# A fused audio tower: the tokenizer's end in another order, its last stores waited for later, and 127 unread TensorE turns

## The reference

```python
def reference(x, ...):
    h = _L0_tok_ref(x, W, b, gamma, beta)            # 16x16 patches @ W + b, then layernorm
    h = h + _L0_attn_ref(_layernorm(h), Wq, Wk, Wv, Wo, bo)   # 16 heads of 64, rope, causal
    h = h + _L0_ffn_ref(_layernorm(h), router_w, router_b, w1, w3, w2)   # 4 experts, top 2, silu
    h = h + _L1_attn_ref(_layernorm(h), phazor...)   # linear recurrence over time
    h = h + _L1_ffn_ref(_layernorm(h), w_gate, w_up, w_down)  # quantised gated ffn, 256 -> 768 -> 256
    return h
```

## Time and profile before

| | |
|---|---|
| median of 3 runs | 1666.11 us (1664.1 to 1670.38) |
| the profiled execution's own time | 1669.95 us |
| its span | 1668.1 us |
| TensorE matmul busy | 1444.7 us, 87% of the span |
| VectorE, ScalarE, GpSimd busy | 1183.3, 952.9, 873.5 us |

### The profile page before, as it was taken

How to read it: one execution, slowest core, us unless ns; L and a number is a source line. 1 busy time by engine, 2 the same in 40 slices (tenths; PEclk the granted TensorE clock), 3 DMA queues, 4 the chain that set the end, 5 groups by cost and what they waited for, 6 DMA issues and landing times. The chain is left out here.

```text
span 1668.1 us, 30233 instructions
## 1 busy us (share of the span) xinstructions
PE 1444.7 (87%) x10725; PEld 1359.9 (82%) x10725; DVE 1183.3 (71%) x2575; ACT 952.9 (57%) x2102; POOL 873.5 (52%) x721
## 2 busy tenths in 40 slices
PE   5379999999999999996599999999998847799049
PEld 4269999999999989996499999999998846798039
DVE  6648788888888888784346666666578379459886
ACT  4637676767676767674254444445443335459642
POOL 4458586969686868581355554555544523023000
PEclk8679999999999999998699999999999968899569
DMA  7391202121212120000576766666665331003403
GB/s 254 131 316 54 77 20 83 33 83 33 83 33 83 33 71 17 27 14 29 180 239 191 215 180 193 195 203 203 174 208 156 79 96 47 10 16 124 157 19 112
DMA packets 91427, 186.36 MB, mean 112 GB/s; under 512 B 8997, under 2 KB 64301, under 8 KB 91021
## 3 DMA queue, kind: packets, MB, share of 16 engines
q1 hardware_dynamic: 80765, 170.75, 30.9%
q0 software_dynamic: 10512, 13.68, 4.8%
HBM read 138.57 MB, written 58.91 MB: 118 GB/s over the span
## 5 line engine op out<-in xcount | busy, mean ns | idle before, releaser
L1664 POOL TENSOR_TENSOR expert_w<-expert_raw,expert_w 128x768 fp32r<-128x768 f32 x95 | 182.2, 1918 | 237.5 <-ACT expert_w L1486 237.5
L1444 PE MATMUL psum<-slots_high,expert_w 128*128 128x376 f32 x1216 | 288.5, 339 | 7.2 <-DVE expert_act L1630 5.9
L887 ACT ACTIVATE expert_raw<-psum,neg_max 120x376 f32<-120x376 f32 (+2 forms) x384 | 176.6, 486 | 95.9 <-DVE neg_max L1090 95.9
L1444 PEld LDWEIGHTS psum<-slots_high,expert_w 128*128 128x128 f32 x1216 | 210.6, 190 | 11.4 <-issue 9.6
L1524 ACT ACTIVATE expert_act_high<-expert_act 128x376 fp32r<-128x376 f32 x152 | 78.8, 518 | 181.6 <-DVE expert_act L1630 181.6
L1113 DVE TENSOR_TENSOR pt_low<-psum,pt_high 128x752 fp32r<-128x752 f32 x128 | 120.5, 941 | 81.3 <-ACT pt_high L896 81.1
L1455 PE MATMUL psum<-expert_w,expert_act_high 128*128 128x256 f32 x912 | 172.0, 285 | 3.2 <-ACT slot_out L1506 3.0
L1635 DVE TENSOR_TENSOR expert_act_low<-expert_act,expert_act_high 128x376 fp32r<-128x376 f32 x152 | 110.5, 727 | 79.0 <-ACT expert_act_high L1524 79.0
L1009 POOL TENSOR_TENSOR qk_low<-rotated,qk_high 128x376 fp32r<-128x376 f32 x128 | 126.7, 990 | 66.8 <-ACT qk_high L880 66.7
L1444 PE MATMUL psum<-slots_low,expert_w 128*128 128x376 f32 x608 | 155.5, 337 | 0.0
L1455 PEld LDWEIGHTS psum<-expert_w,expert_act_high 128*128 128x128 f32 x912 | 144.0, 186 | 6.1 <-ACT slot_out L1506 5.7
(11 more groups left out here) (308 smaller groups left out, 3993.6 us busy)
## 6 DMA issues: line engine op xcount, KB each, us to landing
expert_w<-experts_split SPq DMA_DIRECT2D x57, 768.0 KB, 4.3
expert_raw<-in_experts SPq DMA_DIRECT2D x95, 384.0 KB
x_slots<-in_c_slots SPq DMA_DIRECT2D x4, 3102.0 KB
up_spill<-held SPq DMA_DIRECT2D x5, 1128.0 KB, 5.0
held<-up_spill SPq DMA_DIRECT2D x5, 1128.0 KB, 5.8
slot_rows<-x_slots SPq DMA_DIRECT2D x19, 264.0 KB, 4.1
whole_w<-in_experts SPq DMA_DIRECT2D x12, 384.0 KB, 4.5
experts_split<-pt_high SPq DMA_DIRECT2D x12, 384.0 KB
```

The source lines that it names most:

```text
L887: last = act.activation(probs[0:ni, h % 2, at:at + P * it + ni], score_bank(h % 2, it), ACT.Exp, bias=neg_max[0:ni, h % 2, it:it + 1], acc ...
L1444: last = pe.matmul(psum[:, 2 * k + g % 2, 0:TILE_SLOTS], w[hw][:, f, at:at + P], xt[hx][:, i % 2, c, :], start=(n == c == 0), stop=(n == 2 ...
L1664: pool.tensor_tensor(w[1][:, g % RING, :], raw[:, r % RAW, :], w[0][:, g % RING, :].bitcast(F32), ALU.subtract).then_inc(w_low, 1)
```

## The change

Four edits. SP issues the store of turned rows ahead of the store of h in each iteration. VectorE does `x_low` of the clips 4 to 7 last in its iteration, after the statistics and the inverse of the clip that is two behind, and the casts of `masks` after the statistics. The block of the tokenizer no longer ends with waits for its last stores: SP waits for them at the head of attention's block, and ScalarE and VectorE ahead of their first write into `pt` (L896, L1113). And TensorE gets 127 turns of the identity matrix into a part of PSUM that nobody reads, at five places (18, 9, 70, 16 and 14).

```diff
+def keep_running(pe, psum, ident, bank, times):
+    for _ in range(times):
+        pe.transpose(psum[:, bank, TOK:TOK + P], ident[:], ident[:])
...
                 for i in range(BATCH + 4):
+                    if 2 <= i - 4 < BATCH:
+                        u = (i - 4) % 2
+                        sp.wait_ge(x_kept, i - 3)
+                        sp.dma_start(x_dram[:, :, :, tokens_of(i - 4)], xt[:, u, :, :, :].bitcast(F32)).then_inc(x_stored[u], 16)
                     if here(i):
                         sp.wait_ge(h_made, i + 1)
...
-                    if 2 <= i - 4 < BATCH:
-                        u = (i - 4) % 2
-                        sp.wait_ge(x_kept, i - 3)
-                        sp.dma_start(x_dram[:, :, :, tokens_of(i - 4)], xt[:, u, :, :, :].bitcast(F32)).then_inc(x_stored[u], 16)
-                for u in range(2):
-                    sp.wait_ge(x_stored[u], 16 * (BATCH // 2 - 1))
                 sp.wait_ge(tables_in, 16 * 10)
-                for b in range(BATCH - 3, BATCH):
-                    sp.wait_ge(stored[b % 3], 32 * (b // 3 + 1))
...
-                    if here(i - 4):
+                    if here(i - 4) and here(i):
                         x_low(i - 4)
-                    if i == BATCH:
-                        masks()
                     if here(i - 2):
                         dve.wait_ge(h_made, i - 1)
                         stat(1, i - 2, h[:, (i - 2) % 3, :, :])
+                    if i == BATCH:
+                        masks()
                     if here(i):
                         inverse(0, i, h_scaled)
                     if here(i - 2):
                         inverse(1, i - 2, x_made)
+                    if here(i - 4) and not here(i):
+                        x_low(i - 4)
...
+        def front_stored(engine):
+            for u in range(2):
+                engine.wait_ge(x_stored[u], 16 * (BATCH // 2 - 1))
+            for b in range(BATCH - 3, BATCH):
+                engine.wait_ge(stored[b % 3], 32 * (b // 3 + 1))
...
             def _(sp):
+                front_stored(sp)
...
+                pe.wait_ge(proj_read, 16 * BATCH + CR_READ)
+                keep_running(pe, psum, ident, BANK_PROJ, 18)
                 pe.wait_ge(pt_ready, 16 * BATCH + CR_PT)
                 pe.wait_ge(inv_kept, 16 * BATCH - 1)
                 turn_rows(LAST, 0)
                 turn_rows(LAST, 1)
                 logit(LAST)
+                keep_running(pe, psum, ident, BANK_PROJ, 9)
                 ahead_of(LAST)
+                keep_running(pe, psum, ident, BANK_PROJ, 70)
...
                 def turned_high(b, h):
...
+                    if b == h == 0:
+                        front_stored(act)
...
                 def turned_low(b, h):
                     dve.wait_ge(pt_high, 16 * b + h + 1)
+                    if b == h == 0:
+                        front_stored(dve)
...
+                keep_running(pe, psum, ident, 0, 16)
                 turn(0, 0)
                 turn(0, 1)
                 up(0)
...
                 share(STEP_X)
+                keep_running(pe, psum, ident, 0, 14)
```

More of the change, by code:

```diff
@@ L84, in attention_tables, with tokens_in @@
         sb("before", [P, P], BF16), sb("ones_b", [P, P], BF16), sb("slot_base", [P, EXPERTS]))}
-def tokens_in(nc, psum, a, consts, ident, vec, decay, first, weights, h0_rows, x_dram, tables, cos, made):
+def tokens_in(nc, psum, a, consts, ident, vec, decay, first, weights, h0_rows, x_dram, tables, cos, stored, x_stored, made):
     ctx, sb, sem = scopes(nc, made)
@@ L111, in tokens_in @@
         arrived = [sem(f"{n}_arrived") for n in matrices]
-        stored = [sem(f"tok_stored{u}") for u in range(3)]
-        x_stored = [sem(f"tok_x_stored{u}") for u in range(2)]
         summed, std_made, rstd_made = ([sem(f"tok_{n}{i}") for i in range(2)] for n in ("summed", "std_made", "rstd_made"))
@@ L441, in attention @@
 def attention(nc, psum, h0_rows, x_dram, weights, a, consts, ident, x_slots, h_rows, onehot, where, shared, raw_w, w_in,
-              split_w, scattered, tables, made):
+              split_w, scattered, tables, stored, x_stored, made):
     ctx, sb, sem = scopes(nc, made)
@@ L2386, in audio_tower @@
         front_sems = []
+        front_stored = [ctx.enter_context(nc.semaphore(f"tok_stored{u}")) for u in range(3)]
+        front_x_stored = [ctx.enter_context(nc.semaphore(f"tok_x_stored{u}")) for u in range(2)]
         early = ctx.enter_context(ExitStack())
@@ L2402, in audio_tower @@
             tokens_in(nc, psum, a, consts, ident, vec, decay, first, weights, h0_rows, x_dram, tables,
-                      shared[:, 4 * TOK:5 * TOK], front_sems)
+                      shared[:, 4 * TOK:5 * TOK], front_stored, front_x_stored, front_sems)
             attention(nc, psum, h0_rows, x_dram, weights, a, consts, ident, x_slots, h_rows, onehot, where, shared,
-                      raw_w, w_in, split_w, scattered, tables, front_sems)
+                      raw_w, w_in, split_w, scattered, tables, front_stored, front_x_stored, front_sems)
         held = ctx.enter_context(nc.sbuf_tensor("held", [P, UPS * QCHUNKS * TOK], F32))
```

## The result

The changed kernel takes 1656.65 us (median of 5 runs, 1655.34 to 1657.1), against 1667.11 (5 runs, 1664.1 to 1670.38) for the kernel before: a ratio of 0.9933 with a 95% interval of 0.9921 to 0.9946, so 0.5 to 0.8% faster. The forecast was 1656.3, in 1652.5 to 1661.5.

What follows compares the result with a forecast made beforehand. TensorE is busy for 87% of the span; the edits sit at four seams between stages, where engines wait. Savings of 7.8 + 0.5 + 0 + 1.5 = 9.8 us from a median of 1666.11 gave 1656.3, range 1652.5 to 1661.5.

Steps and rivals of the forecast that it cites:

- The likeliest case: Whole kernel: the forecast itself, 9.8 us saved, 1656.3 us; chance 0.60.
- The rival of smaller seams: Whole kernel: seams give less, with slow landings and little clock gain; 5.5 us saved, 1660.6; chance 0.17.
- that of larger ones: Whole kernel: landings at 4.0 and the clock up everywhere; 13.4 us saved, 1652.7; chance 0.08.
- Term 1: Tokenizer's last iterations: the new order ends the circular waits, last low part 4.2 us earlier, 3.4 to 5.0 by landings.
- Term 2: Tokenizer's block end: without the store waits attention starts at 78.6, not 86.44; 7.8 us with the new order's saving.
- rival (c): Attention's start: the waits only move, it starts at 82; 1659.9 us; chance 0.05.
- Term 3: Attention's end: turns hold the clock up for logits and rows, 0.5 us saved, bounds 0 and 1.6; 70 turns cost nothing.
- the third: Attention's end: of at most 1.6 us saved, a third was taken, 0.5, because the clock at 785 varies.
- Rival (b): All turns: they don't raise the clock and the 70 cost 3.7 us; 4.1 saved, 1662.0; chance 0.06.
- Rival (d): All turns: writing one PSUM place, each costs its duration, 0.27 us and more; at 0.45, 1689; chance 0.04.
- Term 4: Experts' start: 16 turns are hidden and the third chunk waits for ScalarE; 0 us, bounds gain 0.7, loss 2.5.
- Term 5: FFN's start: 14 turns fill 3.1 us idle, the clock rises 3.1 earlier; 1.5 us saved, bounds 0 and 2.5.

Runs made afterwards that it cites:

- the waits alone: Kernel before with only the moved waits, SP's and VectorE's order as before, no turns: 0.9977 of the kernel before, 1663.81 us.
- the turns alone: Kernel before with only the 127 turns added: 0.9984 of the kernel before, 1664.4 us.
- the pause closed: The change with 8 more turns ahead of the rows' six turns at attention's end: 0.9924 of the kernel before, 1654.11 us.
- the 140 turns: The change with 140 turns in place of the 70 at attention's end: 0.9983 of the kernel before, 1664.1 us.
- the two experiments that have the 14 turns otherwise: Kernel before with only the 127 turns, 1664.4 us; the change without the 113 turns outside the FFN, 1658.14 us.
- the casts at the end: The change with the casts of masks two iterations later, behind clip 6's low part: 0.9927 of the kernel before, 1653.97 us.

## Why the prediction was right

The likeliest case came about: 1656.65 against 1656.3. The rival of smaller seams (1660.6) and that of larger ones (1652.7) did not. That it was met to 0.35 us is in part luck: the kernel before came out 1.0 slower in the five runs than in the three the forecast started from, and two errors in term 1 cancelled. By its own steps:

**Term 1**, 4.2 forecast up to the end of the last low part, 3.9 measured. The replay was right in what is late next, and wrong in two sizes that cancelled. I add 2.25 to the times after, to lay them on the forecast's clock. Clip 6's deviation was forecast at 66.1 and came at 65.9. Then the step "VectorE has done the statistics and the casts by then" failed: I had taken the casts at their durations of before, some 0.9 together, and they took some 3.9, so the scaled rows of clip 6 came at 69.8 and not 68.4. So clip 5's store, forecast at 70.8, could not go out before 71.9, where clip 5's low part ends. The stores gave most of it back: I had taken 4.8 for a landing, the middle of the range in the earlier trace rows, whose median is 4.0, and from SP's issue at 66.78 to ScalarE's start at 70.73 it was 3.95. The last low part ends at 77.7 by the forecast's clock, 0.3 behind the 77.4.

**Term 2**, 3.6 forecast, 3.36 with the waits alone. From the end of the last low part to the memset 1.22 was forecast and 1.46 measured. The whole stretch: 7.8 forecast, 7.28 measured, inside the bounds 7.0 to 8.6. Nothing waited in attention for the stores, so rival (c) is out: the part up to the last projection was 698.12 with the moved waits, 698.78 before.

**Term 3**, 0.5 forecast. The seam itself gave 0.4 in the change's profile (23.74 less 23.34), 0 in the turns alone and up to 1.9 elsewhere, over the bound of 1.6: with the pause closed the logits start 1.46 behind the first of the six turns and not 2.06, so 0.6 is saved there where I had taken 0.4. "Whether the clock is up at 785 differs from one execution to the next" is right: the last projections take 0.41 each in the kernel before and in three others, 0.28 in the rest. But the third was a guess about the wrong side. In all three profiles that had the clock up at the eighteen turns and left the pause open, 2.46 where I forecast 2.4, the logits had lost it. The 70 turns cost nothing: 9.71, where I had worked out 10.2. They ended at 796.1, after GpSimd's last issue but 1.7 ahead of its branch at 797.8, and 1.7 is the cover that the 140 turns used up. I had written that the last of them ends before GpSimd's scatter; it ends before the landings that GpSimd waits for, and that is what counts.

**Rival (b)** rests on the Trainium skill (TensorE: Matmul & The Clock Gate, Part 4: PE-mode transpose). By that rule the window from 791 to 793 had to stand at 0.50, and it shows 1.00 with nothing but turns since 786.38. The measurement decides against it for the instruction that `pe.transpose` gives here. The trace calls that a MATMUL and doesn't show whether the transpose mode that the page speaks of is on. The earlier trace rows were weaker evidence than I took them for: the twelve turns end at 1373.55, and the window 1374 to 1376 holds ordinary matmuls, which had begun at 1373.34.

**Rival (d)** is out: a turn costs 0.11 to 0.12 at full clock, even with 140 into one place.

**Term 4**, 0 forecast, and nothing gained or lost in the change. From the first turn of slot rows to the third chunk it was 9.73 before and is 9.67 after. The six turns are faster (0.87 for 1.52), and ScalarE's transfer and table load take it back, as forecast.

**Term 5**, 1.5 forecast, 1.47 measured in the change, 1.55 and 1.50 in the two experiments that have the 14 turns otherwise. The clock rises 3.2 earlier behind the share's end, for 3.1 forecast.

The terms as measured: 7.3 + 0.4 + 0 + 1.5 = 9.2, and the medians differ by 10.5 with an interval of 9.0 to 13.2 (0.9946 and 0.9921 of 1667.11). The 13.0 between the two profiles hold 2.25 at the start and 1.47 at the end that belong to no edit.

One sum of the forecast is off: with a spread of 2, a distance of 1.5 leaves 0.23 of the 0.60 on the far side, 0.14 and not 0.07, so faster should have stood at 0.54 and same at 0.42.

## What to carry to other kernels

When two queues wait for each other in a circle, replay both with durations from the trace and then ask which resource is late next; the answer was a pair of buffers, and their landings then set what the new order could save. Work that is moved has to be priced beside what runs at its new place: four small casts became four times as long because GpSimd was at work there. Unread work that keeps the clock up pays where it fills a pause completely, as ahead of the FFN. Where a pause of 2.5 us was left behind it, the piece behind the pause still ran slowly, in three profiles of three. Such a gain is judged by its own stretch together with the one ahead of it: a piece that runs at full clock may owe that to a loss just before.

## What the runs showed of the hardware that was not expected

VectorE's copy of 128x4 f32 took 1.78 us and 0.16 without GpSimd, its cast of 128x256 1.89 and 0.28, a scalar_tensor_tensor of 128x3 1.20 and 0.16. Each of the long ones started while a tensor_tensor of GpSimd ran and ended 0.02 to 0.15 behind it. Not every one is held: a reciprocal of 128x3, which started at 63.30 under the same instruction of GpSimd, took 0.17, and the change's cast of 128x128, 0.04 behind the start of GpSimd's first instruction, took 0.19. There GpSimd's own took 1.90, for 1.80 in the kernel with the casts at the end. The Trainium skill (SBUF — State Buffer, SBUF: two separate sides) has the lock that fits: the pair of ports that the two engines share is held for a whole instruction, and VectorE needs it for copies in its faster modes and for two inputs from SBUF. The runs agree in until when the long ones are held, and in the kinds of instruction; that cast of 0.19 shows that an overlap alone is not enough. No run here shows the ports themselves. That it can hit an instruction of three columns on the critical path was what I had not looked for.
